# Two heads' maxima by differences and relu on TensorE, and key tiles read in three pieces, in a gated cross-attention block

## What is computed

```
q = (query @ Wq + bq).reshape(Bq, Sq, H, DK)
k = (key @ Wk + bk).reshape(Bq, Sk, H, DK)
v = (value @ Wv + bv).reshape(Bq, Sk, H, DK)
scores = jnp.einsum('bqhd,bkhd->hbqk', q, k) / np.sqrt(DK)
attn = jax.nn.softmax(scores.reshape(H * Bq, Sq, Sk), axis=0).reshape(H, Bq, Sq, Sk)
out = jnp.einsum('hbqk,bkhd->bqhd', attn, v).reshape(Bq, Sq, H * DK)
```

## Time and profile before

| | us |
|---|---|
| three runs | 843.67, 848.89, 851.2 |
| median | 848.89 |
| profiled execution, its own time | 850.6 |
| its span, first to last instruction | 848.4 |

### The profile page before, as it was taken

One profiled execution on the slowest core, in us unless ns is written; L12 is line 12 of the kernel. 1 busy time (PEld: TensorE's weight loads), 2 busy tenths in 40 slices (PEclk: granted clock), 3 DMA queues, 4 the chain that ended last, 5 costly groups with the idle time before them and its releaser, 6 DMA issues. The chain is left out here.

```text
span 848.4 us, 20088 instructions
## 1 busy us (share of the span) xinstructions
PE 739.7 (87%) x8151; PEld 445.4 (53%) x8151; DVE 757.7 (89%) x825; ACT 680.9 (80%) x1094; POOL 475.1 (56%) x225
## 2 busy tenths in 40 slices
PE   8898896777777769999999999999999999559977
PEld 6564371212222126676767677777666777425334
DVE  4899639899999978999999999999999995758967
ACT  3454449899999979898999999999998934759973
POOL 1333463000000010999999999999999997414500
PEclk9999999999999989999999999999999999879999
DMA  9773579999998628668867896878877794000014
GB/s 296 238 238 113 157 193 237 285 273 269 204 237 189 231 87 249 173 195 273 260 192 219 241 289 205 226 210 276 261 189 202 242 327 140 2 2 1 1 51 148
DMA packets 94987, 165.88 MB, mean 196 GB/s; under 512 B 10160, under 2 KB 37552, under 8 KB 94384
## 3 DMA queue, kind: packets, MB, share of 16 engines
q1 hardware_dynamic: 94896, 164.60, 67.2%
HBM read 142.81 MB, written 42.73 MB: 219 GB/s over the span
## 5 line engine op out<-in xcount | busy, mean ns | idle before, releaser
L1019 POOL TENSOR_TENSOR e<-e,recip 128x1792 f32<-128x1792 f32 (+3 forms) x128 | 367.9, 2920 | 19.2 <-DVE recip L1050 19.2
L971 ACT ACTIVATE e<-psY 128x512 f32<-128x512 f32 x512 | 296.4, 647 | 33.5 <-PE psY L904 27.7
L1037 DVE TENSOR_REDUCE partial<-e 128x128 f32<-128x4096 f32 (+1 forms) x80 | 283.3, 3561 | 6.9 <-ACT e L971 6.9
L904 PE MATMUL psY<-arena 128*128 128x128 bf16 x2048 | 200.4, 221 | 0.0
L904 PEld LDWEIGHTS psY<-arena 128*128 128x128 bf16 x2048 | 149.0, 98 | 73.7 <-issue 26.7
L707 ACT ACTIVATE copies<-ps_max 128x1024 bf16<-128x1024 f32 x189 | 175.7, 1058 | 3.3 <-PE ps_max L686 3.3
L900 PE MATMUL psY<-shift,minus 128*128 128x512 bf16 x396 | 152.9, 386 | 10.5 <-PEq L641 5.5
L723 DVE TENSOR_TENSOR high<-copies,high 128x3072 bf16<-128x3072 bf16 x63 | 110.1, 1747 | 0.4 <-ACT copies L707 0.4
L1010 POOL MEMSET ones_w<- 96x128 bf16 x1 | 0.2, 207 | 176.1 <-POOLq L641 176.1
L718 DVE TENSOR_TENSOR high<-ps_max,high 128x1024 bf16<-128x1024 f32 x63 | 76.6, 1216 | 4.9 <-PE ps_max L686 4.9
L920 PE MATMUL psX<-e,arena 128*32 128x128 f32 x2048 | 76.5, 288 | 2.3 <-issue 1.3
(11 more groups left out here) (173 smaller groups left out, 1008.2 us busy)
## 6 DMA issues: line engine op xcount, KB each, us to landing
arena<-k_stack SPq DMA_DIRECT2D x264, 256.0 KB, 3.3
arena<-q_stack SPq DMA_DIRECT2D x64, 256.0 KB, 4.4
arena<-in_x_dram SPq DMA_DIRECT2D x8, 1024.0 KB, 10.3
k_stack<-parts SPq DMA_DIRECT2D x24, 256.0 KB, 3.1
q_stack<-parts SPq DMA_DIRECT2D x24, 256.0 KB, 3.0
k_stack<-k_stack SPq DMA_DIRECT2D x4, 1536.0 KB, 20.5
q_stack<-q_stack SPq DMA_DIRECT2D x4, 1536.0 KB, 15.4
arena<-in_ctx_dram SPq DMA_DIRECT2D x4, 1024.0 KB, 6.2
```

Of the source, the lines that this page charges most:

```text
L904: last = nc.tensor.matmul(bank[:, j * P:(j + 1) * P], ks[:, i % KRING, b * P:(b + 1) * P], qs[:, h, b * P:(b + 1) * P], start=False, stop= ...
L971: nc.scalar.activation(e_at(p, half * HB, (half + 1) * HB).rearrange("p q z i -> p z q i"), ps[n % SCORES][:].rearrange("p (z q i) -> p z ...
L1019: nc.gpsimd.tensor_tensor(part, part, by_pairs(recip[:, r % 2, :], share), ALU.mult).then_inc(pool_scaled, 1)
L1037: nc.vector.tensor_reduce(partial[:, :, k, :], e[:, t:t + n].rearrange("p t q z i -> p q i t z"), AX.XY, ALU.add).then_inc(sum_done, 1)
```

## The change

*Maxima.* A couple and one batch are now a group; there are again 64. The odd heads' keys are stored negated: `permute` scales the odd columns of `wk` by -1 in a second ACTIVATE, and VectorE makes a sign vector and multiplies `bk_s` by it, for which ScalarE waits ahead of its first bias (`bias_signed`). In 128 rows `k_mixed` then gives the difference d = even score - odd score, and the larger of two scores is relu(d) + odd score. For the chunks 0 to 2 TensorE writes d to `ps_x` (3 banks), ScalarE writes relu(d) as bf16 to `gain` (one ACTIVATE of 1024 columns and one of 512), and TensorE writes minus the odd score and adds minus the gain, with `minus` as weights, to `ps_y` (3 banks); VectorE takes minima from PSUM into `lowest` (512 and 1024 columns). Chunk 3 isn't done so: even and negated odd score go to `ps_c` (2 banks), ScalarE copies both (1024 columns), and VectorE merges the copies of two groups in two operations of 1024 bf16 columns, one a group. At the end three small operations fold the last rows. The maxima are kept negated, so that even heads add them with a new matrix `plus` and odd heads with `minus`, and the exponential of odd heads has a negative scale. `load_couple` loads 14 pieces for a couple where 10 were loaded before: a third set of key pieces, for three chunks, is new. `ident_b` becomes `plus`, and `zero_w` a column of `vpad`.

*Stacks.* `k_stack` keeps its 48 written rows only. The key copies from DRAM to DRAM are gone (8 DMAs, 10 MB); those of the queries stay (8 DMAs, 10 MB). Each key tile of attention is read by `load_keys` in three DMAs: rows 0 to 47, again 0 to 47, and 0 to 31 of `k_stack`, to 48, 48 and 32 partitions.

```diff
-K_COPIED = (((3, 6), (0, 3)), ((6, 8), (0, 2)))
+K_READ = ((0, 3), (0, 3), (0, 2))
-COPIES_OF_COUPLE = (2, 2, 3, 2, 3, 2, 2, 0)
+QUERY_COPIES = [(c, *rows) for c in range(4) for rows in Q_COPIED]
+COPIES_OF_COUPLE = (2, 1, 1, 1, 1, 1, 1, 0)
+
+def load_keys(sp, k_stack, kc, h, tile, loaded):
+    at = 0
+    for first, n in K_READ:
+        sp.dma_start(tile[at:at + n * DK], k_stack[kc, h, first * DK:(first + n) * DK, :]).then_inc(loaded, 16)
+        at += n * DK
...
+    rows(mixed[0:HALF], k_stack, 2 * p, K_MAX_ROWS)
+    rows(mixed[HALF:P], k_stack, 2 * p + 1, K_MAX_ROWS, NC - 1)
+    for j in range(2):
+        rows(both[j * HALF:(j + 1) * HALF], q_stack, 2 * p + j, Q_MAX_ROWS)
+    rows(odd[HALF:P], k_stack, 2 * p + 1, K_MAX_ROWS)
...
-                permute(wk_p, wk_s, "wk_loaded")
+                permute(wk_p, wk_s, "wk_loaded", (1.0, -1.0))
...
+                act.wait_ge(s["bias_signed"], 1)
...
+                dve.wait_ge(s["sign_set"], 2)
+                nc.vector.tensor_scalar(bk_s[:], bk_s[:], sign[:, 1:2], None, ALU.mult).then_inc(s["bias_signed"], 1)
...
+                def differences(g):
...
+                    for kc in range(MIXED):
+                        if g:
+                            pe.wait_ge(gained, 2 * (g - 1) + (2 if kc == MIXED - 1 else 1))
+                        nc.tensor.matmul(ps_x[:, kc, :], keys(k_mixed, g, kc), queries(g), start=True, stop=True
+                                         ).then_inc(x_scored, 1)
+                def plain(g):
+                    if g:
+                        pe.wait_ge(c_copied, g)
+                    for j, tile in enumerate((k_mixed, k_odd)):
+                        last_mm = nc.tensor.matmul(ps_c[:, j, :], keys(tile, g, MIXED), queries(g), start=True, stop=True)
+                    last_mm.then_inc(c_scored, 1)
+                def smaller(g):
+                    for kc in range(MIXED):
+                        if g:
+                            pe.wait_ge(y_merged, 2 * (g - 1) + (1 if kc == 0 else 2))
+                        nc.tensor.matmul(ps_y[:, kc, :], keys(k_odd, g, kc), queries(g), start=True, stop=False)
+                        pe.wait_ge(gained, 2 * g + (2 if kc == MIXED - 1 else 1))
+                        nc.tensor.matmul(ps_y[:, kc, :], minus[:], gain[:, g % RING, kc, :], start=False, stop=True
+                                         ).then_inc(y_scored, 1)
+                for g in range(GROUPS):
+                    differences(g)
+                    plain(g)
+                    if g:
+                        smaller(g - 1)
...
                         nxt = (i + KRING) % STEPS
-                        sp.dma_start(ks[:, nxt % KRING, :], k_stack[nxt // H, nxt % H]
-                                     ).then_inc(k_loaded[nxt % KRING], 16)
+                        load_keys(sp, k_stack, nxt // H, nxt % H, ks[:, nxt % KRING, :], k_loaded[nxt % KRING])
```

More of the change, by code:

```diff
@@ L106, with load_couple, rows @@
 EARLY_ITEMS = SCORES + 1
[L109 to L116, removed]
+COUPLE_PIECES = 3 * len(K_MAX_ROWS) + 2 * len(Q_MAX_ROWS)
+def load_couple(sp, p, k_stack, q_stack, mixed, odd, both, loaded):
+    def rows(tile, stack, h, plan, chunks=NC):
         at = 0
         for first, n in plan:
-            sp.dma_start(tile[at:at + n * DK], stack[:, h, first * DK:(first + n) * DK, :].rearrange("c p x -> p c x")
+            sp.dma_start(tile[at:at + n * DK, 0:chunks],
+                         stack[0:chunks, h, first * DK:(first + n) * DK, :].rearrange("c p x -> p c x")
                          ).then_inc(loaded, 16)
             at += n * DK
[L123 to L129, removed]
+    rows(mixed[0:HALF], k_stack, 2 * p, K_MAX_ROWS)
[3 more added lines that the diff above has]
+    rows(odd[HALF:P], k_stack, 2 * p + 1, K_MAX_ROWS)
 def prepare(nc, sem, x, ctx_in, wq, bq, wk, bk, wv, bv, wg, wu, wd, k_stack, q_stack, keep):
@@ L142, in prepare @@
         ident = sb("ident", [P, P])
-        ident_b = sb("ident_b", [P, P], BF16)
+        ident_b = keep["plus"]
+        sign = sb("sign", [P, 2])
         diag = sb("diag", [P, DC, P])
@@ new lines, in _ @@
+                for g in range(GROUPS):
+                    for n, (k0, k1) in enumerate(((0, 1), (1, MIXED))):
+                        dve.wait_ge(y_scored, MIXED * g + k1)
+                        if g:
+                            dve.wait_ge(y_merged, 2 * (g - 1) + n + 1)
+                            nc.vector.tensor_tensor(lowest[:, k0:k1, :], ps_y[:, k0:k1, :], lowest[:, k0:k1, :], ALU.min
+                                                    ).then_inc(y_merged, 1)
+                        else:
+                            nc.vector.tensor_copy(lowest[:, k0:k1, :], ps_y[:, k0:k1, :]).then_inc(y_merged, 1)
+                    if g > 2:
+                        merge((g - 1) // 2, (g - 1) % 2)
@@ new lines, in _ @@
+                merge(GROUPS // 2 - 1, 1)
+                merges = 2 * (GROUPS // 2 - 1)
+                dve.wait_ge(c_merged, merges)
+                for j, op in enumerate((ALU.max, ALU.min)):
+                    nc.vector.tensor_tensor(folds[:, j, :], last[:, j, 0, :], last[:, j, 1, :], op).then_inc(c_merged, 1)
+                dve.wait_ge(c_merged, merges + 2)
+                nc.vector.scalar_tensor_tensor(out=lowest[:, MIXED, :], in0=folds[:, 0, :], scalar=-1.0, in1=folds[:, 1, :],
+                                               op0=ALU.mult, op1=ALU.min).then_inc(folded, 1)
```

201 lines of the change are left out of this document (95 added, 106 removed).

## The result

| | before | after |
|---|---|---|
| runs, us | 843.67, 848.89, 851.2, 847.62 | 907.52, 910.69, 908.13, 905.36 |
| median, us | 848.25 | 907.83 |
| ratio, with its 95% interval | | 1.071 (1.068 to 1.074) |
| span of the profiled execution, us | 848.4 | 905.7 |

What follows compares the result with a forecast made beforehand. DVE and ACT bound the maxima, DVE and POOL attention, where SP's issues would become the bound. From 850.6 us, maxima -21, prepare +0.5 and attention +28 gave 858 us; range 832 to 884, likeliest case 848 to 870.

Steps and rivals of the forecast that it cites:

- The ordinary issue: Attention, SP's queue: back-to-back issues follow each other at 0.47 us, so 832 of them are 391 us.
- the term for issues of 1 us and more: Attention, SP's queue: some issues take 1 us and more (up to 1.17); 8 us put for those in 832.
- DVE's lead and SP's residual waits: Attention: taken off the added time, 3 us that DVE's lead absorbs and 2 us where SP still waits.
- The reserve: Attention: SP's 225.7 us of waiting for scores, set against 237 us for two more issues in each of 252 steps.
- Rival A: Attention: SP doesn't become the bound, pieces issue at 0.42 us or less; 831 us in all, chance 0.18.
- Rival C: Attention: issues and landings slower under load, SP at 0.52 us or more on the mean; 900 us, chance 0.12.
- Rival B: Maxima: nothing gained, three engines wait in turn and a group stays near 2.8 us; 879 us, chance 0.12.
- the longest loop: Maxima: from one copy of `ps_c` through PE and ACT work with three hand-offs, 4.9 us for two groups, 2.45 each.
- the change to the second couple: Maxima: the first couple's change-over, 3.9 us before because query pieces landed behind DRAM copies; 2 us kept (0 to 6).
- the vanished key copies: Maxima: dropping them gives nothing further, since they ran beside the scoring and only one wait showed them.
- Prepare: Stage before maxima: ACT's first bias waits for DVE's sign, DVE's following work slips 1.6 us; 0.5 us taken (0 to 2).
- four more pieces end before the stage does: Prepare: the first couple's four additional loads finish before the stage ends, as do 0.9 us more of zeros on POOL.

## Why the prediction was wrong

**The bound was named rightly.** SP's issue time was to become what attention waits for, and it did: all that the prediction said would show it is there. SP's waits fell under 40 us (33.8 by the view, 3.8 by the updates that the tiles need), TensorE's for key tiles rose above 40 (67.6 in the weight loads alone), VectorE waits for ScalarE and GpSimd for VectorE. The ordinary issue was sized well, 0.465 us against 0.47; 832 of them alone would be 387 us.

**The step that failed is the term for issues of 1 us and more.** It was put at 8 us, from a maximum of 1.17 in the earlier trace rows. There were 51, with 1.37 us in the mean, 0.95 above an ordinary one: 48 us, 40 more than forecast, of the 45 by which SP's stretch overran (438.9 against 391 + 8 - 5 = 394). The row had been read as the tail of a distribution that grows with the number of issues. It has a cause with a clock of its own: one issue is hit for nearly each of the packets on the instruction queue, of which there are as many as before. Before, they fell into SP's idle time or beside an issue behind a pause, which is seldom hit. The same row hid it, since a maximum doesn't tell how many, and 225.7 us of waits covered them. The remaining 5 us of the overrun are the 5 taken off for DVE's lead and SP's residual waits, which didn't come back, and 4.2 us of idle gaps, less the 4 us that the ordinary issues came out below.

**The reserve was compared as a sum, and that is wrong in the other direction too.** By sums, one added issue a step costs nothing; it cost 17 us as a tiny DMA, and 20 as a second piece, part of which is that piece's later landing. Between 328 issues (0), 580 (+17, +20), 784 (+59) and 832 (+71, and +76 with the old maxima) no threshold shows. The lateness is that of single tiles. The forecast did weigh the tiles' slack, but gave it no term of its own.

**Rival A** (SP isn't the bound) falls: the pieces' issues take 0.422 us in the median and follow each other at 0.465, above the 0.44 at which A begins, and the 0.32 of before belonged to issues behind a wait, as the prediction held. The Trainium skill's sentence in "DMA: Bandwidth & Descriptors", "Issuing engines are not separate DMA queues", that the time to initiate is "usually small relative to the DMA itself", doesn't decide here: 0.42 against 2.2 us to landing is small for one, and 832 of them, one after the other, are 387 of attention's 467 us. **Rival C** had the place and nearly the size (900 us): SP at 0.528 us per issue on the mean is its case, though not by load on the DMA engines, whose share fell.

**Rival B** (the maxima gain nothing) falls. VectorE's row of merges in the changed kernel:

```profile
L756 DVE TENSOR_TENSOR last<-copies,last x62: 679/681/684, 138.1 to 292.0; 128x1024 bf16<-128x1024 bf16 x62
```
```profile
249.62 0.68 DVE L756 TENSOR_TENSOR last<-copies,last 128x1024 bf16<-128x1024 bf16 x1
...
251.99 0.68 DVE L756 TENSOR_TENSOR last<-copies,last 128x1024 bf16<-128x1024 bf16 x1
...
254.55 0.68 DVE L756 TENSOR_TENSOR last<-copies,last 128x1024 bf16<-128x1024 bf16 x1
```

The groups are 2.37 and 2.56 us apart in turn, 2.48 over the stage without its one long wait, where 2.45 was forecast. All three engines are 91 to 94% busy (154.6, 155.3 and 160.6 us of 170.5). The stage took 170.5 us in place of 166. Some 2 us are the 0.03 in 64 groups, and that was in the prediction's own terms: those of the longest loop add up to 4.95 us and not 4.9, which is 2.48 a group. (Its ends, 5 and 3 us less a group, are 5.5, where the 164 has 7 in it; the two slips cancel.) The other 2.6 us are the change to the second couple, which cost 4.6 us where 2 was kept; in four other kernels with new maxima and fewer copies than before it cost 1.5 to 4.1:

```profile
150.90 0.69 DVE L764 TENSOR_TENSOR lowest<-ps_y,lowest 128x512 bf16<-128x512 f32 x1 [4.64 <-PE ps_y L717]
```

**That the vanished key copies give nothing** held for the old maxima, 183.4 us without them and 183.4 to 186.9 with them. For the new ones it is wrong: they turn 179.0 us into 170.5. A shorter stage must move the same bytes faster, and the stage's DMA share was 0.89 already.

**Prepare.** VectorE's sign cost nothing that shows: prepare's last computation ends at 120.4 us, before at 124.7, and from 121.1 to 125.6 in the others. But "four more pieces end before the stage does" failed: they and the stack writes share full DMA engines, and a gap of about 4 us stands ahead of the first score in every kernel that has them. (They are 14 where prepare loaded 10; a whole couple of the kernel before had 12, the odd head's 2 among them, and not the 10 of "The change".) In this pair of executions it is masked by the earlier end.

In all: maxima -16.4 (forecast -21), attention +71.1 (forecast +28), start -0.8 and the rest +3.4.

## What to carry to other kernels

Splitting a DMA costs its issue on a queue that works in series, and the queue is not free just because it waits much of the time: compare the added issues with the slack of each single transfer, and expect a loss before the queue is full. Count how many issues in the trace are far above the median and when they come, not only the largest one; what is rare in a queue that mostly waits may be tied to something periodic, and be met every time once the queue never rests. Before a stage that also carries copies is made shorter, check whether its DMA share leaves room for the same bytes in less time. And before a few us of a stage are put down to a change, look how long the same stage took in other profiles that left it alone.

## What the runs showed of the hardware

- Issues on SP's queue that overlapped a 16 KB packet on the instruction queue took up to 1.8 us instead of 0.42 in the changed kernel: all 49 such packets of its key tile loads met one of over 0.6 us. In the kernel without computation 21 of 400 issues were long beside 19 packets, 8 beside 6, and 2 beside none, these two beside packets of 8 KB.
- An issue that began within 0.3 us of such a packet's start was long in 275 of 366 cases when it followed another issue at once, and in 17 of 86 behind a pause of over 0.1 us (twelve kernels).
- An issue's cost depends on its form and on what stood ahead of it: 0.30 to 0.32 us behind a wait, 0.42 back to back, 0.49 to 0.59 for 1 KB from DRAM to DRAM, and 0.58 for a key tile between two of those.
- DMAs of 96 and 64 KB to part of the partitions landed in 2.2 and 2.3 us in the median, one of 256 KB to all 128 in 3.3, in the same stage of two kernels. But one of 160 KB to 80 partitions took 3.5, and tiles in two or three pieces were whole after 4.00 and 3.58 us.
